# A convolution followed by window attention on one core: q is computed for two tiles at once with the divided projection, and TensorE's loop begins at another place of the turn

## The reference

```
x = x + conv3x3(group_norm(x))
x = x + attention(group_norm(x))
```

```
q = relu(q); k = relu(k); v = [v, 1]
kv = k^T v                      # 8 x 9 per window and head
o  = q kv;  o = o[:8] / (o[8] + 1e-15)
```

## Time and profile before

| what | value |
|---|---|
| median of 3 runs | 2421.53 us (2421.18 to 2421.76) |
| the profiled execution | 2419.14 us |
| its span, first to last instruction | 2417.3 us |
| mean granted TensorE clock | 0.999 |
| TensorE busy | 2366.7 us, 98% |
| VectorE, ScalarE, GpSimd busy | 1730.8, 1451.0, 1170.9 us |
| DMA, mean over the span | 24 GB/s |

### The profile page before, as it was taken

One profiled execution on the slowest core, in us unless ns is written; L12 is line 12 of the kernel. 1 busy time (PEld: TensorE's weight loads), 2 busy tenths in 40 slices (PEclk: granted clock), 3 DMA queues, 4 the chain that ended last, 5 costly groups with the idle time before them and its releaser, 6 DMA issues.

```text
span 2417.3 us, 112385 instructions
## 1 busy us (share of the span) xinstructions
PE 2366.7 (98%) x49576; PEld 2150.9 (89%) x49576; DVE 1730.8 (72%) x3206; ACT 1451.0 (60%) x3754; POOL 1170.9 (48%) x2365
## 2 busy tenths in 40 slices
PE   7999999999999999999999999999999999998998
PEld 7998899888998889988899888998889988897887
DVE  9887658767587765877658766687766876665764
ACT  2158861588516884178832788327882288813886
POOL 0037750477405773057730677216771167712776
PEclk9999999999999999999999999999999999999999
DMA  4000010000200001000010000100001000000000
GB/s 171 1 2 16 19 65 10 2 19 16 75 1 6 15 20 71 1 6 19 16 71 1 7 18 16 71 1 9 16 20 66 1 9 19 21 9 2 16 16 25
DMA packets 39114, 58.37 MB, mean 24 GB/s; under 512 B 4704, under 2 KB 36064, under 8 KB 36832
## 3 DMA queue, kind: packets, MB, share of 16 engines
q1 hardware_dynamic: 38880, 55.27, 6.4%
HBM read 29.57 MB, written 25.69 MB: 23 GB/s over the span
## 4 chain that ended last, share of the span: by engine, by line
PE 95%; DVE 2%; issue 1%; DMA 0%; ACT 0%; SPq 0%; POOL 0%; POOLq 0%; DVEq 0%
PE ps L354 33%; PE ps L425 15%; PE ps L373 12%; PE ps L414 10%; PE ps L400 9%; PE ps L380 9%; PE ps L389 4%; PE ps L434 3%; DVE dp L883 1%; DMA xs<-w_conv 0%; PE ps L336 0%; DVE xs L896 0%; DVE kv_part L989 0%; PE ps L365 0%; DVE rcp L999 0%
## 5 line engine op out<-in xcount | busy, mean ns | idle before, releaser
L354 PE MATMUL ps<-dp,wc 128*128 128x392 f32 x4608 | 840.8, 341 | 0.2 <-DVE dp L883 0.2
L354 PEld LDWEIGHTS ps<-dp,wc 128*128 128x128 f32 x4608 | 815.3, 188 | 5.3 <-issue 3.1
L1204 POOL TENSOR_TENSOR ve<-vpraw,vmask 128x1024 f32<-128x1024 f32 x200 | 381.0, 1905 | 349.8 <-ACT vpraw L665 349.8
L425 PEld LDWEIGHTS ps<-at,wp 128*128 128x128 f32 x3200 | 373.1, 191 | 47.5 <-DVE kvm L1016 46.4
L425 PE MATMUL ps<-at,wp 128*128 128x128 f32 (+1 forms) x3200 | 404.7, 280 | 1.0 <-ACT yb L700 1.0
L1175 POOL TENSOR_TENSOR qm<-qraw 128x64 f32<-128x64 f32 x200 | 59.5, 298 | 700.5 <-ACT qraw L672 699.9
L636 ACT CAST dp<-dt 128x896 fp32r<-128x896 f32 x128 | 121.0, 945 | 449.0 <-PE ps L354 356.3
L373 PE MATMUL ps<-wkv,xt 128*128 128x512 f32 x1200 | 324.8, 406 | 1.6 <-issue 1.6
L654 ACT ACTIVATE ve<-ps,vmask 128x256 f32<-128x256 f32 x800 | 314.3, 491 | 0.0
L414 PEld LDWEIGHTS ps<-kvm,qs 64*32 64x32 f32 x25088 | 233.5, 105 | 90.8 <-issue 88.8
L1016 DVE TENSOR_TENSOR kvm<-ps,hm 128x576 f32<-128x576 f32 (+1 forms) x400 | 277.4, 734 | 2.9 <-PE ps L400 2.8
(11 more groups left out here) (86 smaller groups left out, 3110.3 us busy)
## 6 DMA issues: line engine op xcount, KB each, us to landing
out<-xs SPq DMA_DIRECT2D x224, 112.0 KB, 1.8
xs<-x SPq DMA_DIRECT2D x14, 1344.0 KB, 7.5
xs<-x SPq DMA_DIRECT2D x14, 224.0 KB, 2.7
xs<-w_conv SPq DMA_DIRECT2D x2, 1152.0 KB, 12.2
xs<-x SPq DMA_DIRECT2D x2, 896.0 KB, 6.6
xs<-x SPq DMA_DIRECT2D x2, 672.0 KB, 7.8
kvm<-w_kv SPq DMA_DIRECT2D x1, 512.0 KB, 13.7
wp<-w_proj SPq DMA_DIRECT2D x4, 128.0 KB, 9.9
```

Of the source, the lines that this page charges most:

```text
L354: last = nc.tensor.matmul(ps[:, conv_bank(v, mt), 0:CONV_N], wc[:, part_w, k, kt * TAPS + dy, mt * P:(mt + 1) * P], dp[:, kk % 2, part_d, ...
L425: last = nc.tensor.matmul(ps[:, BANK_A + mt, Y0:Y0 + n], wp[:, q, mt * P:(mt + 1) * P], at[:, q, e, 0:n], start=(q == 0), stop=(q == QUADS ...
L1204: nc.gpsimd.tensor_tensor(ve[:, t % 2, :, 1].rearrange("p e (n m) -> p e n m", m=DIM + 1)[:, :, :, 0:DIM], vpraw[:].rearrange("p (n m) -> ...
```

## The change

- **q for pairs.** `q_of_pair` takes the place of `q_of_tile` on TensorE: 256 tokens of two tiles at once, as a divided product (12 instructions of 256 columns). It reads xt, whose layout now puts two tiles of one channel half side by side; wq is held as high and low part. The last tile of an image, alone in its pair, is done with 64 columns. The result fills BANK_Q; ScalarE copies it to qraw for both tiles, and takes the two tiles' relu and mask from qraw. GpSimd pools a pair in one pass. q_done, qraw_ready and qsum_ready count pairs.
- **The loop turned round.** `tile` is cut in two: `small_arrays` (attend, keys times values) and `whole_array` (all the rest). The loop's body is now whole array, small arrays, whole array, small arrays, for turns 2 to 21; the branch back stands behind the small arrays.
- **The projection** goes to BANK_Q. In even turns (s even) the order is q of the pair, transposes, pooled, project, keys_values; in odd turns project first half, transposes, pooled, project second half, keys_values. It waits for qraw_ready or y_ready, no longer for masked.
- **The last turns.** In turn 23 projection and transposes come ahead of the convolution's half; in turn 24 the half stays ahead of the transposes. Two convolution products use other banks.
- **ScalarE's order** in even turns: pooled_q, q_of_pair, turned, pooled_keys_values, q_of_tile, batch_norm; in odd turns: q_of_tile, turned, pooled_keys_values, pooled_q, batch_norm; then as before. At an image's start, q of pair 0 is computed before keys and values of tile 1.
- The slots of the code are set anew; there is one ahead of turn 1's whole array.

```diff
-LOOPED = TILES - 5
-FIRST_LOOPED = 1
-SLOT_LEAD, SLOT_FIRST, SLOT_LOOP, SLOT_OUT = 152, 80, 92, (80, 56)
+PAIRS_Q = -(-TILES // 2)
+LOOPED = TILES - 5
+FIRST_LOOPED = 2
+SLOT_LEAD, SLOT_LOOP, SLOT_OUT, SLOT_LAST, SLOT_SECOND = 160, 236, 215, 171, 255
...
-            def q_of_tile(e):
+            def q_of_pair(tokens=2 * TT):
                 for mt in range(MT):
-                    for kt in range(KT):
-                        last = nc.tensor.matmul(ps[:, BANK_Q, mt * TT:(mt + 1) * TT],
-                                                wq[:, kt, mt * P:(mt + 1) * P], xh[:, e, kt, :],
-                                                start=(kt == 0), stop=(kt == KT - 1))
+                    for i, (part_w, part_x) in enumerate(PARTS):
+                        for kt in range(KT):
+                            last = nc.tensor.matmul(
+                                ps[:, BANK_Q, mt * 2 * TT:mt * 2 * TT + tokens],
+                                wq[:, part_w, kt, mt * P:(mt + 1) * P],
+                                xt[:, part_x, kt, :, :].rearrange("p e t -> p (e t)")[:, 0:tokens],
+                                start=(i == 0 and kt == 0), stop=(i == len(PARTS) - 1 and kt == KT - 1))
                 last.then_inc(q_done, 1)
...
-            def project(e, units):
+            def project(e, units, mts=range(MT)):
...
-                        last = nc.tensor.matmul(ps[:, BANK_A + mt, Y0:Y0 + n],
+                        last = nc.tensor.matmul(ps[:, BANK_Q, mt * TT:mt * TT + n],
...
+            def whole_array(T, pair, e, s=None, v=None):
...
+                if half and s == 0:
+                    pe.wait_ge(qraw_ready, pairs - 1)
+                    product(*half)
+                if e == 0:
+                    if is_tile(2) and s != 0:
+                        if is_tile(3):
+                            pe.wait_ge(xh_low, n4)
+                        pe.wait_ge(y_ready, n0)
+                        q_of_pair(2 * TT if is_tile(3) else TT // 2)
+                elif is_tile(-1):
+                    pe.wait_ge(qraw_ready, pairs)
+                    if is_tile(-2):
+                        pe.wait_ge(y_ready, n0)
+                    project(1 - e, 2, (0,) if is_tile(2) else range(MT))
+                if half and s == TILES - 1:
+                    product(*half)
                 pe.wait_ge(ao_ready, n1)
                 turn(units(0))
+                if half and s == TILES - 2:
+                    pe.wait_ge(masked, masks)
+                    product(*half)
                 if is_tile(2):
                     pooled(n3)
+                if e == 1 and is_tile(-1) and is_tile(2):
+                    project(1 - e, 2, (1,))
+                if s == 0:
+                    if half:
+                        pe.wait_ge(conv_added, 2 * v + 4)
+                    pe.wait_ge(xh_low, n4)
+                    pe.wait_ge(qraw_ready, pairs - 1)
+                    q_of_pair()
+                if e == 0 and is_tile(-1):
+                    if is_tile(2):
+                        pe.wait_ge(qraw_ready, pairs)
                     else:
                         pe.wait_ge(y_ready, n0)
                     project(1 - e, 2)
...
                 with pe.Fori(0, LOOPED // 2) as i:
                     for e in range(2):
-                        tile(t0 + i * 2 + (FIRST_LOOPED + e), (FIRST_LOOPED + e) % 2)
+                        t = FIRST_LOOPED + e
+                        whole_array(t0 + i * 2 + t, p0 + i + t // 2, t % 2)
+                        small_arrays(t0 + i * 2 + t + 1, (t + 1) % 2)
...
                 if t >= 2:
                     act.wait_ge(kv_done, b * TILES + t - 1)
-                nc.scalar.copy(xt[:, 0, t % 2], xh[:, t % 2]).then_inc(xh_high, 1)
+                    act.wait_ge(q_done, b * PAIRS_Q + t // 2)
+                nc.scalar.copy(xt[:, 0, :, t % 2, :], xh[:, t % 2]).then_inc(xh_high, 1)
...
+            def q_of_pair(b, i):
+                n = 2 * TT if 2 * i + 1 < TILES else TT // 2
+                act.wait_ge(q_done, b * PAIRS_Q + i + 1)
+                if i >= 1:
+                    act.wait_ge(qsum_ready, b * PAIRS_Q + i)
+                nc.scalar.copy(qraw[:].rearrange("p (m n) -> p m n", m=MT)[:, :, 0:n],
+                               ps[:, BANK_Q, :].rearrange("p (m n) -> p m n", m=MT)[:, :, 0:n]).then_inc(qraw_ready, 1)
...
-            nc.scalar.copy(wkv[:, 0], wkv_raw).then_inc(att_w_high, 1)
+            nc.scalar.copy(wkv[:, 0], wkv_raw)
+            nc.scalar.copy(wq[:, 0], wq_raw).then_inc(att_w_high, 1)
...
-                    dve.wait_ge(q_done, b * TILES + t - 1)
                     dve.wait_ge(xh_high, b * TILES + t - 1)
```

More of the change, by code:

```diff
@@ L436, in turn, with small_arrays @@
                     last.then_inc(tr_done, 1)
-            def tile(T, e, s=None, v=None):
+            def small_arrays(T, e, s=None):
                 def is_tile(d):
@@ L446, in units @@
                     return 2 if s is None else tile_units(s + d)
-                n0, n1, n2, n3, n4 = [held(pe, T + d) for d in range(5)]
-                masks, own_mask = held(pe, T * 2 + 2), held(pe, T * 2 + 3)
+                n0, n1, n2 = [held(pe, T + d) for d in range(3)]
+                masks = held(pe, T * 2 + 2)
                 pe.wait_ge(w_loaded, DMA)
@@ L467, in tile, with is_tile, units @@
                     keys_times_values(1, 1 - e, units(1))
+            def whole_array(T, pair, e, s=None, v=None):
+                def is_tile(d):
+                    return s is None or 0 <= s + d < TILES
+                def units(d):
+                    return 2 if s is None else tile_units(s + d)
+                n0, n1, n2, n3, n4 = [held(pe, T + d) for d in range(5)]
+                masks, pairs = held(pe, T * 2 + 2), held(pe, pair + 1)
                 half = None if v is None else {0: (v - 1, 1), TILES - 3: (v, 0), TILES - 2: (v, 1),
@@ L520, in attention @@
                     pe.wait_ge(conv_added, 2 * v + 3)
-                else:
-                    at_slot(SLOT_FIRST)
-                for s in range(FIRST_LOOPED):
-                    tile(t0 + s, s % 2, s, v)
+                first = FIRST_LOOPED + LOOPED
+                small_arrays(t0, 0, 0)
+                whole_array(t0, p0, 0, 0, v)
+                small_arrays(t0 + 1, 1, 1)
+                at_slot(SLOT_SECOND)
+                whole_array(t0 + 1, p0, 1, 1)
+                small_arrays(t0 + 2, 0, 2)
                 at_slot(SLOT_LOOP)
@@ L527, in attention @@
                     for e in range(2):
-                        tile(t0 + i * 2 + (FIRST_LOOPED + e), (FIRST_LOOPED + e) % 2)
-                for s in range(FIRST_LOOPED + LOOPED, TILES):
-                    if s - FIRST_LOOPED - LOOPED < len(SLOT_OUT):
-                        at_slot(SLOT_OUT[s - FIRST_LOOPED - LOOPED])
-                    tile(t0 + s, s % 2, s, v)
+                        t = FIRST_LOOPED + e
+                        whole_array(t0 + i * 2 + t, p0 + i + t // 2, t % 2)
+                        small_arrays(t0 + i * 2 + t + 1, (t + 1) % 2)
+                for s in range(first, TILES):
+                    if s == first:
+                        at_slot(SLOT_OUT)
+                    whole_array(t0 + s, p0 + s // 2, s % 2, s, v)
+                    if s + 1 < TILES:
+                        small_arrays(t0 + s + 1, (s + 1) % 2, s + 1)
             def last_tile(b):
@@ L750, in first_chunk @@
                 keys_values(b, 0)
-                q_of_tile(b, 0)
                 pooled_keys_values(b, 0)
                 split(v + 4)
+                q_of_pair(b, 0)
                 split_tile(b, 2)
                 keys_values(b, 1)
+                for t in range(2):
+                    q_of_tile(b, t)
                 pooled_keys_values(b, 1)
@@ L1221, in _ @@
             for b in range(B):
+                spread_pooled(b, 0)
                 pool_q(b, 0)
-                spread_pooled(b, 0)
                 spread_pooled(b, 1)
-                for s in range(-1, TILES):
-                    if 0 <= s < TILES - 2:
+                for s in range(TILES):
+                    if s < TILES - 2:
                         spread_pooled(b, s + 2)
-                    if s + 2 < TILES:
-                        pool_q(b, s + 2)
+                    if s % 2 == 0 and s + 2 < TILES:
+                        pool_q(b, s // 2 + 1)
                     if 1 <= s:
```

128 lines of the change are left out of this document (64 added, 64 removed).

## The result

The change made the kernel slower: 2469.51 us median (2466.39 to 2471.66, 5 runs) against 2421.57 (2421.18 to 2424.54, 5 runs) of the kernel before beside it, a ratio of 1.0195 with a 95% interval of 1.0181 to 1.0209. The forecast was 2386 us and the range ended at 2420. The profiled execution took 2470.67 us, its span 2468.9.

What follows compares the result with a forecast made beforehand. TensorE was taken as the bound, busy for 98% of the span. The terms -32.9 - 15.8 + 8 + 2.4 + 6.2 - 3.5 + 0.5 = -35.1 us, from 2421.5, gave 2386 us; range 2362 to 2420.

Steps and rivals of the forecast that it cites:

- The q pairs: q products on TensorE: 12 instructions of 256 columns, 1.40 us a pair, -32.9 us (bounds -38 and +38).
- Rival 4: q products on TensorE: 256 columns cost 0.178 us an instruction, giving 2457 us; chance 0.04.
- The projection's wait: Projection in the loop no longer waits for VectorE's mask read, -15.8 us; its wait for ScalarE's copy hidden by 0.1.
- The branch: Loop's branch back, now behind the small arrays: 0.1 us for each of 80 trips, +8 us (bounds 0 and 0.4).
- rival 1: New small waits in the pair of turns, 0.2 to 0.5 us a pair, 2404 to 2430 us; chance 0.13.
- Fetching code: First passes through the small arrays: as many stalls left, at other offsets; 0, with 8 us either way.
- Rival 2: Branch back behind the small arrays exposes a code fetch, 1.07 us a trip, 2464 us; chance 0.06.
- The odd turn: Keys and values in odd turns wait some 0.07 us for ScalarE, bounds 0 and 0.2; +6.2 us.
- GpSimd's pair: GpSimd pools a pair at once in 4.5 to 4.9 us, hidden by 0.4 us.
- Rival 3: GpSimd's pooling of a pair costs twice a tile's chain, 1.0 us a pair, 2474 us; chance 0.04.
- The last turns: Last two turns of an image: same products in another order, VectorE's three operations still covered; 0.

Runs made afterwards that it cites:

- the run on theory D: The kernel with the branch back behind keys and values, but with the odd turn's whole projection between pooling and keys and values: 2483.59 us, ratio 1.0256.

## Why the prediction was wrong

**The q pairs: mechanism right, size a little off.** Forecast 1.40 us for twelve instructions behind another whole-array piece; measured 1.45 (1.63 with the switch, 1.60 forecast), 0.12 an instruction where the proportion gave 0.1165. That is +0.03 to +0.05 a pair, some 4 us of the 32.9. Rival 4 (0.178) is refuted. (The lower bound of this term was added up wrongly: 0.07 us for each of 96 pairs makes it -39.6, not -38; nothing hangs on it.)

**The projection's wait: gone,** and so is the wait for kvm in the weight loads. L428 takes 1.82 us for sixteen instead of 1.79, and the list has a wait for qraw of 16.4 us over 78 weight loads, 0.2 at the longest. I had costed that wait as hidden by 0.1 us; it costs about 0.03 a pair.

**The branch: the first step that failed.** I let the array's change-over of 0.20 us and the sequencer's lead hide all but 0.1 of 0.4 to 0.5 us. Neither hid much: 0.37 us of issue stand ahead of the q pair, which then still takes 1.66 us, change-over included. Over 80 trips that is 30 us for the 8 taken, within my own bound of 0.4. The row was there, 384 rows in 2.3 us, and I took a quarter of the bound without a reason. With the 0.37 the forecast would have been 2408, still inside the range: this step alone would not have sunk it. The forecast for the pair without the branch was about 14.64 us; the run with the branch back has 14.76, and 14.87 as a mean, for once an image VectorE's normalization comes 1 us late in the shorter turns. That late result is rival 1 in small.

**Fetching code: the step that decided.** I wrote "0, with 8 us either way", by counting first passes. Their number was right and the reasoning wrong: a first pass does not cost a fixed 1.07 us; its gaps went from nothing to 2.6 us in the changed kernel and 3.5 in the runs, by where the block's end falls and what ran ahead of it. The entry alone became 53.4 us longer. With gaps of 2 us comes a cost that the forecast did not have, the lower clock: 25 us more of full speed missing than before. The balance over the span: issue +62 us (branch 30, late code and the mask below the rest), clock +25, and against it some 36 us that the new order saves (of the 45.5 forecast, branch and jumps left out); the 36 is what is left over, not measured by itself. Rival 2, the loop turned round, gave the right sign and nearly the right time (2464), but by another sum: the trip costs 0.37 us, not 1.07, and no packet of code comes in the steady loop. Its break-even of 0.54 us a trip was not reached; the ends did the rest. By the Trainium skill ("Runtime: NRT & Kernel Launch", "Instruction fetch mechanics") the crossing of a block is mostly hidden; it is not here, the traces show 1.9 us at one.

**The odd turn:** keys and values take 1.53 us where 1.40 and a wait of 0.07 were forecast; 0.13, inside the bounds. 88 x 0.06 is 5 us more. With the whole projection ahead of them they take 1.39 (the run on theory D).

**A cover that I moved away.** Before, the first attention of an image had q of a tile (1.09 us) and keys and values (1.38) between it and the keys times values whose mask it needs. After, only keys and values, 1.61, and 0.68 us of issue at 762.64. The sequencer's wait at the attention, for that mask (L456: ns min/median/max):

```profile
L456 PEldq EVENT_SEMAPHORE  x8: 51/2396/2410, 158.4 to 2264.2; - x8
```

Line 456 names the wait for qs, but the profile has VectorE's mask (kvm, L1081) done at 763.12 and that qs (L719) at 759.94, so it is the mask. The gap is 0.68 to 0.81 us in the first seven images, 5.1 us in all: 0.7 of the 1.2 us ahead of the first turn, and 4.4 in "rest". Without slots it stands the same, 0.72 to 0.73 us, in three images with no packet of instructions near. (Of the +5.1 of "rest", 3.6 lie between the images and 1.5 behind the last one's turn 24.) The prediction had listed q of pair 1 as moved and had not asked what it covered.

**GpSimd's pair** takes 4.75 us (809.87 to 814.62), inside the 4.5 to 4.9 forecast, and is hidden: ScalarE's pooled q waits for it eight times, 2.1 us in all. Rival 3 is refuted. The last turns, exit, are 13.2 us shorter, which the forecast had put at the pairs' share and 0; 5.7 us of it are issue that fell (7.2 to 1.5 us).

## What to carry to other kernels

When a kernel's TensorE work is a dense stretch of small instructions, price each move by what the sequencer has ahead of it: here the same branch cost 0.23 to 0.33 us behind small arrays and nothing visible behind keys and values. An offset of code is a tuned quantity of the whole program: after any edit that adds or removes instructions, the gain must be judged with the gaps at first passes counted apart, as steady loop, entry and exit, and the missing clock apart from the gaps. And a product that is moved takes its cover away from every wait that it stood over, also where it stood only once an image.

## What was not expected of the hardware

At the gaps of the changed kernel a block of instructions took 0.9 to 1.5 us to come, and work went on 1.2 to 1.6 us after it; most such gaps are 1.5 to 2.2 us. A branch back (0.208 us) behind small arrays costs 0.37 us of TensorE's time with everything in place. In the third image two gaps of 1.9 us, 7 us apart, were followed by 3.4 us at 1.2 GHz, which is 1.7 us lost on top of 3.8; a single gap of 1.56 us was followed by 6.8 us at that level (3.4 us lost) in one exit, while single gaps of 0.8 to 1.4 us in the kernel before were not followed by it. What decides is not shown. No set of offsets among the sixteen tried with the new order was faster than the kernel before (lowest ratio 1.0014, 1.0004 to 1.0025); whether one exists that gives the 16 us of the steady loop and keeps the ends is left open.
